# Exact FP4 codes for five of eleven down groups in a decoder layer: two matmul passes instead of three, and a rescale of the PSUM sum on VectorE

## The chip, the cores and the metric

The kernel runs on one core of one Trainium2 chip. The metric is the device time of the whole program in microseconds (us); below, PE is TensorE, DVE is VectorE, ACT is ScalarE, POOL is GpSimd and SP is SyncE, whose queue here issues every DMA.

## The reference

One decoder layer for x of shape (8, 256, 512), with three parts. The third part is the one that the change touches.

```
attention (linear, sigma = elu + 1, with a memory M, z)  -> x1 = layernorm(x + out)
Toeplitz convolution of k*v products of ctx, times q     -> x2 = layernorm(x1 + out)
ffn:
  vals = FP4_LUT[4-bit codes]                # 0, .5, 1, 1.5, 2, 3, 4, 6 and their negatives
  w    = vals * scale[group of 128 inputs, output]
  h    = silu(x2 @ w_gate.T) * (x2 @ w_up.T) # 1408 hidden values = 11 groups of 128
  y    = h @ w_down.T                        # 512 outputs
  y    = y * rsqrt(mean(y^2) + 1e-6);  out = layernorm(x2 + y)
```

A down weight is thus an FP4 code times a scale that is shared by the 128 hidden values of one group and differs for each of the 512 outputs.

## The kernel before

**Precision by passes.** TensorE multiplies fp16. An fp32 value is split into a high and a low fp16 part. For gate and up the weights are kept as exact FP4 codes in fp16 (`wg_hi`), so each product takes two passes (`x2_hi`, `x2_lo`), and between the four input groups ACT multiplies the sum that stands in PSUM by the ratio of two scales (`rescale_sums`, steps `rsI_P`). For down the scaled weight itself is split into `wd_hi` and `wd_lo`, and each group takes three passes of 512 columns (lines 1297, 1298 and 1299): h_hi with wd_hi, h_hi with wd_lo, h_lo with wd_hi. All 11 groups of a token half add up in one PSUM bank without an interruption.

**Stages.** The tokens of the second and third part go in eight blocks of 256 (two halves of 128). The start stage does the attention of all tokens, prepares the weights (33 tiles: POOL unpacks one, `wsN`; PE flips it, `wN`; ACT writes the high part, `whN`; for down tiles DVE writes the low part, `wlN`), and already runs the body of the first block. Then the body runs for it = 2 to 7, and a last body ends the program. A body works on the convolution of block it, on the ffn of block it-1, and on the rest of the ffn of block it-2.

**Orders.** Each engine runs its steps in an order written out as a string; an engine waits at a step until its semaphores are there, and everything behind it in the string waits with it. The body's orders are `PE_ORDER`, `DVE_ORDER`, `ACT_ORDER`, `POOL_ORDER`; `START_...` and `LAST_...` are those of the start stage and of the last body. The step names that matter here:

- PE: `gI_P` gate and up sums of hidden group I, input group P (4 matmuls of 256 columns); `cU` convolution unit U (3, 6, 9 or 12 matmuls of 288 columns), `d0 d1` the units 0 and 1 of the next block; `yT_I` down group I of token half T (T = 1 belongs to the block before); `w1_I` the same for half 1 in the last body; `ct`, `rt`, `xt` flips of 128x128 blocks.
- DVE: `tmU` products with a convolution unit, five instructions (from line 239); `lk`, `ln` the low part of the kv products (line 216); `kq` a transpose (line 223); `guI` hidden values (line 1201); `bsT`, `bnT`, `nmT`, `xtT` residual sum, statistics, normalisation and low part of x2; `aT`, `bT`, `eT` mean square, residual with statistics, and final normalisation (lines 1207, 1216 to 1224, 1232).
- ACT: `rsI_P`, `guI` (silu), `hhI` (high part of h), `hoT` (copy of x2), `nT` (squares of y).
- POOL: `hlI` (low part of h), `pr`, `pn` (kv products from line 197), `tr` (sums of the terms).

**Waits around the change.** `cU` waits until `tm` of unit U-2 has emptied its bank. `g0_0` waits for both `xt` of DVE. `d0` waits for `ln`. `yT_I` waits for `hlI` and, for I = 0, for `bT` of the block before. `hh` may overwrite a group of h once the down matmuls of the block before have read it.

## Time and profile before

| | |
|---|---|
| median of 3 runs | 537.16 us (536.99 to 537.49) |
| span of the profiled execution, first to last instruction | 535.3 us |
| PE busy | 508.7 us (95%), 3676 instructions |
| ACT busy | 415.7 us (78%) |
| POOL busy | 394.7 us (74%) |
| DVE busy | 374.4 us (70%), 1145 instructions |
| mean granted TensorE clock | 0.995 of full speed |

The profile gives of its own execution's time only the span; the median of the runs lies 1.9 us above it. Times of a trace count from the first instruction. A matmul's duration runs to the modelled end of its pipeline, and the next one starts before that, so what a matmul costs a full PE is the distance from its start to the next start. The same holds, in a smaller degree, for short instructions of DVE and ACT.

In this trace the start stage takes 0 to 176.1 us, the bodies it = 2 to 7 start at 176.10, 226.93, 278.14, 329.34, 380.54 and 431.74, and the last body runs from 481.92 to the last matmul's end at 525.22; then the last rows are normalised and stored.

### The profile page before, as it was taken

What the parts mean: (1) busy time and instruction counts of PE and PEld (TensorE: products, weight loads), DVE (VectorE), ACT (ScalarE), POOL (GpSimd) and SP (SyncE); (2) the same over time, 40 slices, a digit from 0 to 9 for tenths busy, and PEclk for the clock granted to TensorE, in tenths of its full rate; (3) what the DMA queues carried; (4) which work ended last, traced back from release to release, by engine and by line L of the source; (5) the groups of instructions that cost most, each with busy time, mean ns of one, the idle gap of its engine ahead of it and who ended that gap; (6) DMA issues with size and microseconds to landing.
All of it is one profiled execution on the core that took longest, in us unless ns stands there. A gap on an engine that the chain in (4) does not pass through costs nothing.

```text
span 535.3 us, 11768 instructions
## 1 busy us (share of the span) xinstructions
PE 508.7 (95%) x3676; PEld 377.6 (71%) x3676; DVE 374.4 (70%) x1145; ACT 415.7 (78%) x994; POOL 394.7 (74%) x449
## 2 busy tenths in 40 slices
PE   8888899998999999999999999999999999999992
PEld 5676787777785777677767776777677767765660
DVE  2886668988787667776777776768777777763223
ACT  4577875277999788788888897889788877788981
POOL 2768864994898499769968995899589859871231
PEclk9999999999999999999999999999999999999997
DMA  8713776443250862032104210411040111001001
GB/s 224 203 39 63 169 142 180 128 80 99 87 112 24 159 127 86 23 100 79 60 1 117 59 59 0 118 59 59 13 130 14 39 33 49 0 1 42 1 21 39
DMA packets 66146, 40.63 MB, mean 76 GB/s; under 512 B 37882, under 2 KB 55418, under 8 KB 66106
## 3 DMA queue, kind: packets, MB, share of 16 engines
q1 hardware_dynamic: 66106, 40.13, 29.6%
...
## 4 chain that ended last, share of the span: by engine, by line
PE 36%; POOL 27%; issue 19%; ACT 5%; DVE 4%; SPq 4%; DMA 2%; POOLq 1%; DVEq 0%; ACTq 0%
POOL shared L297 9%; POOL h_lo L1102 5%; SPq L415 4%; POOL kv L197 3%; PE p_cv L137 3%; PE p_cv L139 3%; PE p_cv L138 3%; PE p_n L1299 3%; PE p_n L1297 3%; PE p_n L1298 3%; POOL shared L299 2%; PE p_x L1284 2%; PE p_x L1286 2%; PE p_qk L1284 2%; PE p_qk L1286 2%
## 5 line engine op out<-in xcount | busy, mean ns | idle before, releaser
L1102 POOL TENSOR_TENSOR h_lo<-w,h_hi 128x256 f16<-128x256 f32 x88 | 73.6, 842 | 44.6 <-ACT h_hi L1151 43.0
L137 PE MATMUL p_cv<-kv_hi,toe 128*128 128x288 f16 x320 | 91.6, 286 | 1.3 <-DVE shared L257 1.3
L139 PE MATMUL p_cv<-kv_hi,toe 128*128 128x288 f16 x320 | 91.5, 286 | 0.0
L138 PE MATMUL p_cv<-kv_lo,toe 128*128 128x288 f16 x320 | 91.5, 286 | 0.0
L1134 ACT ACTIVATE p_qk<-p_qk,rescale 128x256 f32<-128x256 f32 x192 | 78.3, 451 | 12.5 <-PE p_qk L1286 11.9
L297 POOL TENSOR_TENSOR shared<-shared 128x1024 f32<-128x1024 f32 x32 | 76.8, 2399 | 8.9 <-DVE shared L257 8.8
L1134 ACT ACTIVATE p_x<-p_x,rescale 128x256 f32<-128x256 f32 x192 | 78.4, 452 | 6.2 <-PE p_x L1286 6.0
L1134 ACT ACTIVATE p_s<-p_s,rescale 128x256 f32<-128x256 f32 x144 | 59.0, 456 | 11.2 <-PE p_s L1286 11.1
L1297 PE MATMUL p_n<-wd_hi,h_hi 128*128 128x512 f16 x176 | 66.8, 379 | 0.0
L1298 PE MATMUL p_n<-wd_lo,h_hi 128*128 128x512 f16 x176 | 66.7, 379 | 0.0
L1299 PE MATMUL p_n<-wd_hi,h_lo 128*128 128x512 f16 x176 | 66.7, 379 | 0.0
L1284 PE MATMUL p_qk<-x_hi,wg_hi 128*128 128x256 f16 x256 | 63.0, 273 | 3.6 <-DVE x_lo L285 2.1
L1284 PE MATMUL p_x<-x_hi,wg_hi 128*128 128x256 f16 x256 | 62.9, 273 | 0.7 <-ACT p_x L1134 0.2
L1286 PE MATMUL p_x<-x_lo,wg_hi 128*128 128x256 f16 x256 | 62.8, 273 | 0.0
L1286 PE MATMUL p_qk<-x_lo,wg_hi 128*128 128x256 f16 x256 | 62.8, 273 | 0.0
L239 DVE TENSOR_TENSOR shared<-p_cv,qv 128x128 f32<-128x128 f32 x128 | 36.1, 282 | 32.4 <-PE p_cv L139 31.8
L216 DVE TENSOR_TENSOR kv_lo<-kv,kv_hi 128x1152 f16<-128x1152 f32 x32 | 52.6, 1642 | 3.4 <-ACT kv_hi L180 3.4
L242 DVE TENSOR_TENSOR shared<-p_cv,qv 128x128 f32<-128x128 f32 x128 | 49.7, 388 | 0.0
L299 POOL TENSOR_TENSOR shared<-shared 128x512 f32<-128x512 f32 x32 | 47.7, 1492 | 2.5
L1284 PE MATMUL p_s<-x_hi,wg_hi 128*128 128x256 f16 x192 | 47.1, 273 | 0.9 <-ACT p_s L1134 0.9
L1286 PE MATMUL p_s<-x_lo,wg_hi 128*128 128x256 f16 x192 | 47.1, 273 | 0.0
L180 ACT CAST kv_hi<-kv 128x1152 f16<-128x1152 f32 x32 | 37.3, 1166 | 10.9 <-POOL kv L208 7.2
...
## 6 DMA issues: line engine op xcount, KB each, us to landing
...
```

Of the source, the lines that this page charges most:

```text
L137: nc.tensor.matmul(dst, hi, kh, start=(mb == 0), stop=False)
L138: nc.tensor.matmul(dst, hi, kl, start=False, stop=False)
L139: done = nc.tensor.matmul(dst, lo, kh, start=False, stop=(mb == lb))
L297: nc.gpsimd.tensor_tensor(T[:, :, 0:256], T[:, :, 0:256], T[:, :, 256:512], ALU.add).then_inc(cv.tree, 1)
L299: nc.gpsimd.tensor_tensor(T[:, :, 0:128], T[:, :, 0:128], T[:, :, 128:256], ALU.add).then_inc(cv.tree, 1)
L1102: nc.gpsimd.tensor_tensor(h_lo[:, i, :], h32[:, i % 2, :], h_hi[:, i, :], ALU.subtract).then_inc(h_low, 1)
L1134: done = nc.scalar.activation(sums, sums, ACT.Copy, scale=rescale[:, p - 1, part * GI + i:part * GI + i + 1])
L1284: nc.tensor.matmul(dst, whi, cv.x2_hi[:, k, :], start=(k == 0 and part == 0), stop=False, skip_group_check=True)
L1286: done = nc.tensor.matmul(dst, whi, cv.x2_lo[:, k, :], start=False, stop=True, skip_group_check=True)
L1297: nc.tensor.matmul(p_y[t][:], h_hi[:, i, c], wd_hi[:, i, :], start=(i == 0), stop=False)
L1298: nc.tensor.matmul(p_y[t][:], h_hi[:, i, c], wd_lo[:, i, :], start=False, stop=False)
L1299: done = nc.tensor.matmul(p_y[t][:], h_lo[:, i, c], wd_hi[:, i, :], start=False, stop=(i == GI - 1))
```

## The change

For the down groups 0 to 4 (`EX = 5`) the weight stays an exact FP4 code. The pass with `wd_lo` is gone for them. Since the codes carry no scale, the sum in PSUM has to be brought from the scale of one group to that of the next: DVE multiplies the whole bank (128x512) by a tile of ratios, once after each of the groups 0 to 4, in a new step `sT_I` (`ST_I` in the last body), and `yT_I` for I = 1 to 5 waits for it. The last of these factors is the scale of group 4 itself, so from group 5 on the sum is in true units.

```diff
+        def rescale_down(f, t, i):
+            dve.wait_ge(y_part[t], f * EX + i + 1)
...
+            nc.vector.tensor_tensor(p_y[t][:], p_y[t][:], keep["early"][:, i * D:(i + 1) * D], ALU.mult).then_inc(y_rescaled[t], 1)
         def down(f, t, i):
...
+            if 0 < i <= EX:
+                pe.wait_ge(y_rescaled[t], f * EX + i)
+            nc.tensor.matmul(p_y[t][:], h_hi[:, i, c], wd_hi[:, i, :], start=(i == 0), stop=False,
+                             skip_group_check=True)
+            if i >= EX:
+                nc.tensor.matmul(p_y[t][:], h_hi[:, i, c], wd_lo[:, i - EX, :], start=False, stop=False,
+                                 skip_group_check=True)
+            done = nc.tensor.matmul(p_y[t][:], h_lo[:, i, c], wd_hi[:, i, :], start=False,
+                                    stop=(i < EX or i == GI - 1), skip_group_check=True)
+            if i < EX:
+                done.then_inc(y_part[t], 1)
```

The ratios are made in the start stage by four small DVE instructions (`dr0`), written to memory element by element by one DMA (`rw0`), and read back to all 128 partitions by another (`rl0`, 1.3 MB):

```diff
+        def down_ratios():
+            dve.wait_ge(scales_kept, 2)
+            nc.vector.tensor_scalar(dn_abs[:], sc_d[:, 0:EX], 0.0, NO_SCALE, ALU.is_equal, ALU.mult).then_inc(
...
+            nc.vector.reciprocal(dn_rec[:], dn_abs[:, 1:EX]).then_inc(ratios_made, 1)
...
+            elif name == "rw":
+                sp.wait_ge(ratios_made, 4)
+                sp.dma_start(ratio_rows.rearrange("g (t p) -> p g t", p=P), dn_abs[:],
+                             allow_slow_non_contiguous=True).then_inc(ratios_stored, 16)
+            elif name == "rl":
...
+                sp.dma_start(early[:, 0:EX * D].rearrange("p (g d) -> p g d", g=EX), bass.AP(ratio_rows.tensor, 0, [[0, P], [D, EX], [1, D]])).then_inc(
+                    keep["in_ratio"], 16)
```

For the five weight tiles 22 to 26 the start stage treats codes as it does for gate and up: POOL copies bytes instead of multiplying by the scale, PE flips one 128x128 block instead of four, and DVE has no low part to make (`wl22` to `wl26` are gone). Two waits that keep order inside one buffer are added, in `deviations` (ACT) and `add_residual` (DVE). The tile of ratios takes over the space of buffers that only the start stage uses.

All order strings are written anew. Those of a body, where the steps are most often run:

```diff
-    PE_ORDER = ("y1_0 g0_0 g1_0 y1_1 g0_1 y1_2 ct0 g1_1 g0_2 y1_3 y1_4 g2_0 g0_3 c2 g1_2 g3_0 c3 y1_5 g2_1 g1_3 g3_1 "
...
-                "g8_2 y0_2 g9_0 y0_3 g10_0 g8_3 g9_1 y0_4 g10_1 g9_2 d0 rt1 y0_5 g10_2 g9_3 y0_6 d1 g10_3 xt0 y0_7 "
-                "y0_8 y0_9 xt1 y0_10").split()
-    DVE_ORDER = ("tm0 tm1 gu0 lk1 tm2 tm3 gu1 tm4 tm5 gu2 lk2 tm6 tm7 tm8 gu3 tm9 tm10 lk3 tm11 gu4 a1 tm12 gu5 tm13 "
-                 "kq0 tm14 tm15 b1 gu6 gu7 ln kq1 bs0 bn0 bs1 bn1 gu8 nm0 gu9 nm1 gu10 xt0 xt1 a0 b0 e1 e0").split()
+    PE_ORDER = ("g0_0 g1_0 y1_0 g0_1 g2_0 g1_1 ct0 g0_2 g1_2 y1_1 g0_3 c2 g2_1 g3_0 y1_2 c3 g2_2 g3_1 g1_3 "
+                "c4 c5 g3_2 y1_3 g2_3 c6 g4_0 g5_0 g3_3 y1_4 c7 y1_5 g4_1 g5_1 y1_6 g4_2 c8 c9 y1_7 y1_8 "
+                "y0_0 g5_2 g4_3 y1_9 g6_0 y1_10 g5_3 c10 c11 g7_0 g6_1 ct1 c12 g8_0 g7_1 c13 c14 g6_2 g7_2 "
+                "c15 g8_1 y0_1 g6_3 g7_3 g8_2 y0_2 g9_0 g10_0 rt0 y0_3 g9_1 g8_3 g10_1 y0_4 rt1 g9_2 g10_2 "
+                "y0_5 g9_3 xt0 g10_3 y0_6 y0_7 y0_8 y0_9 xt1 y0_10 d0 d1").split()
+    DVE_ORDER = ("s1_0 tm0 tm1 gu0 s1_1 tm2 lk1 s1_2 tm3 tm4 gu1 tm5 gu2 s1_3 s1_4 lk2 tm6 tm7 tm8 kq0 tm9 "
+                 "s0_0 gu3 lk3 gu4 a1 gu5 tm10 tm11 tm12 tm13 b1 tm14 tm15 s0_1 gu6 gu7 s0_2 bs0 s0_3 bn0 "
+                 "s0_4 bs1 nm0 gu8 bn1 gu9 gu10 nm1 xt0 ln e1 xt1 a0 b0 kq1 e0").split()
```

In the start stage `fs0` (the gate and up scale factors) moves on DVE from behind `dn0` of the first attention tile to behind `o3` of the fourth; on SP `toe0` moves ahead of `st2`, and `rw0` stands between `st3` and `xq0`. In the last body `ho0` moves on ACT from the first step to near the end; behind the last gate and up step `g10_3`, PE has nine `w` and `y` steps in the old order and ten in the new, as these ends show:

```diff
-               "g10_1 g8_3 g9_2 w1_4 g10_2 w1_5 g9_3 w1_6 g10_3 w1_7 y0_6 w1_8 w1_9 w1_10 y0_7 y0_8 y0_9 y0_10").split()
-    LAST_ACT = ("ho0 rs0_1 rs1_1 rs2_1 tl rs0_2 rs1_2 rs0_3 rs2_2 rs1_3 gu0 rs2_3 hh0 gu1 rs3_1 gu2 rs4_1 rs3_2 hh1 "
...
+    LAST_PE = ("y1_0 g0_0 g1_0 g0_1 g1_1 g0_2 g1_2 g2_0 y1_1 g0_3 g1_3 g2_1 y1_2 g3_0 g4_0 g2_2 y1_3 y0_0 "
...
+               "y0_4 g9_1 g10_1 w1_3 y0_5 g8_2 g9_2 g10_2 w1_4 g8_3 y0_6 g9_3 g10_3 w1_5 w1_6 w1_7 w1_8 w1_9 "
+               "w1_10 y0_7 y0_8 y0_9 y0_10").split()
```

## Rows read from the trace of the kernel before

**Rows 1.** Windows: start stage, body 6, body 7, last body; busy us of each engine.

```profile
0.00:176.10 176.10, 162.35 (x1102) 127.19 (x1103) 131.65 (x387) 125.18 (x272) 128.43 (x164) 1.00 0.50 120
380.54:431.74 51.20, 51.02 (x388) 37.71 (x386) 38.47 (x121) 42.89 (x106) 42.90 (x45) 1.00 0.17 51
431.74:481.92 50.18, 49.57 (x370) 35.65 (x369) 35.17 (x118) 39.92 (x101) 39.70 (x41) 1.00 0.08 22
481.92:525.22 43.30, 41.93 (x276) 26.07 (x274) 12.47 (x28) 36.18 (x98) 10.08 (x16) 1.00 0.07 19
```

**Rows 2.** Timeline of PE: end of body 5, begin of body 6 (start, duration, us).

```profile
379.45 0.60 PE L102 MATMUL p_ct<-ident,shared 128*128 128x128 f32 x4
379.89 0.38 PE L1297 MATMUL p_n<-wd_hi,h_hi 128*128 128x512 f16 x1
...
380.32 0.38 PE L1299 MATMUL p_n<-wd_hi,h_lo 128*128 128x512 f16 x1
380.54 0.38 PE L1297 MATMUL p_n<-wd_hi,h_hi 128*128 128x512 f16 x1
...
381.53 0.28 PE L1284 MATMUL p_qk<-x_hi,wg_hi 128*128 128x256 f16 x1 [0.18 <-DVE x_lo L285]
...
381.98 0.27 PE L1284 MATMUL p_x<-x_hi,wg_hi 128*128 128x256 f16 x1
...
387.63 0.30 PE L137 MATMUL p_cv<-kv_hi,toe 128*128 128x288 f16 x1
...
388.75 0.27 PE L1284 MATMUL p_x<-x_hi,wg_hi 128*128 128x256 f16 x1
```

**Rows 3.** Groups of DVE's instructions by line and shape, whole run (busy us, mean ns).

```profile
L216 DVE TENSOR_TENSOR kv_lo<-kv,kv_hi 128x1152 f16<-128x1152 f32 x32 | 52.6, 1642 | 3.4 <-ACT kv_hi L180 3.4
...
L285 DVE TENSOR_TENSOR x_lo<-p_ct,x_hi 128x512 f16<-128x512 f32 x16 | 11.0, 690 | 12.8 <-ACT x_hi L184 12.7
...
L265 DVE TENSOR_TENSOR shared<-p_ct,xr 128x512 f32<-128x512 f32 x16 | 10.7, 671 | 4.5 <-PE p_ct L102 4.5
```

**Rows 4.** Timeline of DVE: end of body 5, begin of body 6.

```profile
371.60 0.65 DVE L265 TENSOR_TENSOR shared<-p_ct,xr 128x512 f32<-128x512 f32 x1
...
378.51 0.69 DVE L285 TENSOR_TENSOR x_lo<-p_ct,x_hi 128x512 f16<-128x512 f32 x1 [0.22 <-ACT x_hi L184]
380.71 0.69 DVE L285 TENSOR_TENSOR x_lo<-p_ct,x_hi 128x512 f16<-128x512 f32 x1 [1.50 <-ACT x_hi L184]
381.46 0.15 DVE L1207 TENSOR_SCALAR ms<-ss 128x1 f32<-128x1 f32 x1
...
384.24 0.55 DVE L1232 TENSOR_SCALAR fin<-z,mv,rs 128x512 f32<-128x512 f32 x1
385.31 1.40 DVE L1232 TENSOR_SCALAR fin<-z,mv,rs 128x512 f32<-128x512 f32 x1 [0.53 <-POOL rs L1098]
386.63 0.28 DVE L239 TENSOR_TENSOR shared<-p_cv,qv 128x128 f32<-128x128 f32 x1
...
388.37 0.46 DVE L1201 SCALAR_TENSOR_TENSOR w<-p_qk,c_up,w 128x256 f32<-128x256 f32 x1
```

**Rows 5.** Timeline of POOL at the same place.

```profile
385.16 1.27 POOL L197 TENSOR_TENSOR kv<-kT 128x512 f32<-128x512 f32 x1
```

**Rows 6.** Timeline of SP's queue in the start stage.

```profile
72.21 8.19 SPq L415 DMA_DIRECT2D x_blocks<-z  x8
...
83.34 4.90 SPq L426 DMA_DIRECT2D xq<-x_blocks  x2
```

**Rows 7.** Timeline of DVE in the start stage.

```profile
17.02 0.20 DVE L682 TENSOR_SCALAR sc_abs<-sc_g 128x88 f32<-128x88 f32 x1
...
19.88 0.60 DVE L767 SCALAR_TENSOR_TENSOR o<-p_n,coef,loc 128x128 f32<-128x128 f32 x2
...
87.06 0.71 DVE L223 STREAM_TRANSPOSE qv<-xq 128x512 f32<-128x512 f32 x1 [1.14 <-DMA xq<-x_blocks]
```

**Rows 8.** Timeline of ACT: begin of the last body.

```profile
484.50 0.62 ACT L1156 COPY x2hold<-shared 128x512 f32<-128x512 f32 x1 [1.69 <-DVE z L1216]
```

More of the change, by code:

```diff
@@ L39 @@
 RING = 5
+EX = 5
 LATE = ("y1", "n1", "a1", "b1", "e1")
@@ L1037, in periods @@
         "y_done", "y_squared", "y_used", "rr_made", "rs3_made", "fin_made", "y_steps"))
+    y_part, y_rescaled = ([sem(f"{n}{t}") for t in range(GT)] for n in ("y_part", "y_rescaled"))
     def before(i):
@@ new lines, in decoder_layer @@
+    START_SYNC = ("x3 x4 cx2 st0 x5 cx3 tw0 st1 cx4 toe0 x6 st2 st3 rw0 xq0 xq1 xq2 x7 cx5 toe1 xr0 xq3 xr1 "
+                  "toe2 xr2 st4 xq4 toe3 rl0 cx6 toe4 xr3 xq5 cx7 st5 st7 st6 toe5").split()
+    START_PE = ("ze0 Xa0 iw0 Xb0 iw1 iw2 iw3 Q0 V0 S0 M0 Xa1 Xb1 N0 iz0 Q1 T0 f0 w0 Oa0 w1 Ob0 Xa2 w2 S1 w3 "
[9 rows of a table added]
+                "+xt1 +y0_8 +y0_9 +y0_10 +d0 +d1").split()
+    START_DVE = ("ze0 is0 sg0 mk0 ig0 u0 dn0 o0 u1 ra0 sg1 rb0 bm0 mk1 u2 dn1 bn0 dr0 o1 u3 ra1 nb0 rb1 bm1 "
[7 rows of a table added]
+                 "+xt1 +kq1 +a0 +b0 +e0").split()
@@ new lines, in decoder_layer @@
+    ACT_ORDER = ("rv0 rs0_1 rs1_1 rs0_2 rs1_2 rs0_3 rs2_1 tl gu0 rs1_3 hk1 rs2_2 hh0 rs3_1 ho0 ct0 rs3_2 "
+                 "rs2_3 gu1 gu2 rs3_3 rs4_1 hk2 gu3 hh1 hh2 rs5_1 rs4_2 rs5_2 rv1 rs4_3 rs5_3 hk3 hh3 gu4 n1 "
+                 "gu5 hh4 rs6_1 rs7_1 hh5 kn rs6_2 rs7_2 rs8_1 rs6_3 ho1 rs7_3 ct1 rs8_2 gu6 gu7 rs8_3 rs9_1 "
+                 "rs10_1 hh6 hh7 rs9_2 rs10_2 gu8 rs9_3 rs10_3 hh8 gu9 gu10 hh9 xt0 hh10 xt1 n0").split()
+    POOL_ORDER = ("pr1 hl0 pr2 tr0 pr3 hl1 hl2 tr1 hl3 pn hl4 hl5 a1 tr2 tr3 bn0 hl6 hl7 hl8 bn1 hl9 b1 hl10 "
+                  "a0 b0").split()
@@ new lines, in decoder_layer @@
+    LAST_PE = ("y1_0 g0_0 g1_0 g0_1 g1_1 g0_2 g1_2 g2_0 y1_1 g0_3 g1_3 g2_1 y1_2 g3_0 g4_0 g2_2 y1_3 y0_0 "
[3 rows of a table added]
+               "w1_10 y0_7 y0_8 y0_9 y0_10").split()
+    LAST_DVE = ("s1_0 s1_1 gu0 gu1 s1_2 s1_3 s0_0 s1_4 gu2 gu3 gu4 a1 s0_1 b1 gu5 s0_2 S1_0 gu6 gu7 S1_1 "
+                "s0_3 S1_2 s0_4 e1 S1_3 S1_4 gu8 gu9 gu10 A1 B1 a0 b0 E1 e0").split()
+    LAST_ACT = ("tl rs0_1 rs1_1 rs0_2 rs1_2 rs0_3 rs1_3 rs2_1 gu0 gu1 rs2_2 hh0 rs3_1 rs4_1 rs2_3 rs3_2 "
+                "rs4_2 gu2 rs3_3 rs4_3 hh1 hh2 gu3 gu4 rs5_1 hh3 hh4 rs6_1 rs7_1 rs5_2 rs6_2 n1 rs7_2 rs5_3 "
+                "rs6_3 gu5 rs7_3 hh5 gu6 gu7 rs8_1 hh6 rs9_1 rs10_1 hh7 rs8_2 rs9_2 rs10_2 rs8_3 rs9_3 "
+                "rs10_3 gu8 gu9 hh8 ho0 gu10 hh9 hh10 N1 ho1 n0").split()
```

107 lines of the change are left out of this document (61 added, 46 removed), and 51 rows, old and new, of tables (LAST_PE, PE_ORDER, START_ACT, START_DVE).

## The prediction

> **What bounds the kernel now.** I read the windows by stage first. In body 6 PE is busy for 51.02 of 51.20 us, DVE for 38.47, ACT for 42.89 and POOL for 42.90 [rows 1]. So a body is PE's: nothing that another engine saves shows, and every us taken from PE shows, as long as the others keep up. The start stage is different: PE is busy for 162.35 of 176.10 us, so 13.75 us are waits. In the last body PE has 41.93 of 43.30 us and ACT, which first waits, 36.18 [rows 1].
>
> What a pass costs a full PE is read in PE's timeline, not from a duration. A pass lasts 0.38 us to the end of its pipeline, but from 380.32 to 380.54 the next one starts after 0.22 us, and the three from 379.89 take 0.65 us in all [rows 2]. I use 0.215. In the same rows a `g` step costs 0.44 (381.53 to 381.98, rounded down), a flip step 0.44 (379.45 to 379.89), and the nine matmuls of `c2` 1.12, or 0.122 each (387.63 to 388.75) [rows 2].
>
> **What is taken from PE.** A body has ten steps `yT_0` to `yT_4`, one pass less in each: 10 x 0.215 = 2.15 us. There are six bodies: 12.9 us. The last body loses 15 passes, 3.2 us. The start stage loses the five of `y0` (1.1 us) and, in five weight tiles, three of four flips (15 x 0.11 = 1.65 us). All in all 80 passes and 15 flips, 18.9 us. Were PE the bound throughout, this would be the gain, and a body would take 51.2 - 2.15 = 49.05 us.
>
> **What is put on DVE.** Ten multiplies of 128x512 a body. Before has none that writes PSUM. The nearest rows are two with one PSUM input, 671 ns (line 265) and 690 ns (line 285) [rows 3]; from one start to the next an instruction costs some 0.08 less (two convolution units, ten instructions, take 386.63 to 388.37, 0.87 a unit [rows 4]). I take 0.61 behind another instruction and 0.69 where PE waits. DVE's busy time becomes 38.5 + 6.1 to 6.9 = 44.6 to 45.4 of 49.05 us: 91 to 93%. By share it still fits. But each multiply is between two steps of PE, and DVE's queue is strict, so I follow the two queues at the two places where DVE has least room.
>
> **First place: the begin of a body.** DVE must do `a0 b0 kq1 e0` of the block before, then `s1_0`, `tm0`. In the trace DVE ends `xt1` at 381.40, PE starts `g0_0` at 381.53, DVE starts `a0` at 381.46, and `tm0` follows at 386.63, 5.2 us behind `a0` [rows 2, 4]. Of that, 1.4 us is `e0`, which takes 0.55 elsewhere (the instruction before it in the rows) but starts at 385.31, inside POOL's 1.27 us product at 385.16 [rows 4, 5]. The new order has `kq1` in place of `e1`, in the time of a wait for POOL, and the same neighbours on POOL, so the collision stays: `s1_0` starts 4.8 us behind `g0_0` (4.0 without the collision). It ends at 5.5 (4.7). In the new `PE_ORDER` seven `g` steps, a two-pass step and a flip stand ahead of `y1_1`, 7 x 0.44 + 0.43 + 0.44 = 3.95 us. So PE stands still for 1.6 us there (0.75 without the collision). Then `tm0` ends at 6.4, before `c2` needs it. `c5` needs `tm3`, with `tm0` to `tm3`, `gu0`, `lk1`, `s1_1`, `s1_2` ahead; at 0.87, 0.4 (0.46 less 0.08), 1.64 and 0.61 each this can add up to 0.3. In the old order DVE had no `s1_0`, and `tm0` was done at about 387.55, just ahead of `c2` at 387.63 [rows 2, 4]: there was no room to give away.
>
> The Trainium skill, SBUF — State Buffer, "SBUF: two separate sides", says that the port pair shared by VectorE and GpSimd is an exclusive lock that whichever starts first holds for a whole instruction, for VectorE operations in a two-port mode or with two SBUF inputs. The row of `e0` agrees. By this rule the multiply, with one input from PSUM, is never held by POOL and the sums stay as they are; no row of before shows a multiply beside POOL, and were it held as `e0` was, at 0.85 us for a third of the ten, DVE would need 48 us and the slower rival below would be the likeliest.
>
> **Second place: the end of a body.** From `bs0` to the end of `gu10` DVE took 371.60 to 378.51, 6.9 us, of which 0.6 waits that a later start removes: 6.3. The new order puts `s0_3` and `s0_4` into this chain (1.2), then `xt0` 0.65, `ln` 1.64 (the mean of line 216, between 1.3 alone and 2.0 beside POOL), `e1` 0.5, `xt1` 0.69 [rows 3, 4]: 11.0 us, with 0.3 for the flip's end and the way back 11.3. In the old order `ln` and `e1` were not there, and DVE sat idle for 1.50 us ahead of `xt1` [rows 4]. PE from the end of `rt0` to `g0_0` has two two-pass steps, six of three passes, seven `g`, three flips, `d0` and `d1`: 0.86 + 3.88 + 3.08 + 1.32 + 1.10 = 10.2 us. So PE waits up to 1.1 us; with `ln` at 1.3 and the shorter `nm` it is 0.3. I take 0.6.
>
> A body is then 49.05 + 1.6 + 0.6 less 0.3 for small waits that these replace (0.2 of them ahead of `g0_0` [rows 2]) = 50.95 us. Five bodies (it = 2 to 6) gain 0.25 each, 1.2 in sum. Body 7 has no `ln`, `kq` or `d` steps: the second place falls away, and it gains 0.55. The bounds of a body are 49.75 (0.7 and 0.3) and 52.0 (1.9 and 1.1).
>
> **Start stage.** PE's 2.7 us count in part, since it waits for 13.75. On the good side `fs0` moves: its five instructions stood from 17.02 to 19.88 between the denominators and `o0` [rows 7], on the chain of the first tile, 2.9 us; `dr0` comes in its place later with four such small ones, 1 us or, where POOL is in the way as for `fs0`, 3. The five low parts that go save DVE 5 x 0.6 = 3, and `s0_0` to `s0_4` add 3. `s0_1` to `s0_4` stand in a row, with PE steps between them that are too short (`g10_0` only, 0.44, against 1.4 for the multiply and its way): some 1 us. On the bad side is `rw0`. It is 2560 elements of 4 bytes. The nearest rows are the eight issues of `x_blocks`, 4096 rows of 128 bytes, that hold SP for 8.19 us; at this price `rw0` holds it 5.1 us, and it stands ahead of `xq0`, which started at 83.34, about 3 behind the stores, and for which DVE waited 1.14 us at 87.06 [rows 6, 7]. So 2 us of 5.1 lie under the stores' landing, and up to 3 reach `kq0`, and with it the first convolution sums on DVE and POOL. `rl0` is issued long before `s0_0`, which stands late in the body that ends the start stage; it costs nothing, and some 11 us (1.3 MB at the stage's 120 GB/s [rows 1]) if that cover were gone. Together: -2.7 - 2.9 + 1 + 1 + 1.4 (half of what may reach `kq0`) = -2.2, between -5.5 and +3.
>
> The Trainium skill, DMA: Bandwidth & Descriptors, "Rules for kernel authors", says that a last dimension that isn't contiguous becomes one descriptor for each element. It speaks against `rw0`, and agrees with pricing it by count; were it priced by its 10 KB, it would cost nothing, and the start stage would gain 1.4 us more.
>
> **Last body.** ACT goes first to `ho0`, waits for `b0` until 484.50, and only then starts on the rescales, though it was free 1.69 us earlier [rows 8]. With `ho0` (0.5) moved they can start some 2.2 us earlier; the stall at `y1_1` takes 0.7 back (no POOL work collides here). From there ACT has one step after another, so the 3.2 us of PE give nothing more. At the end PE has ten three-pass steps behind `g10_3` instead of nine, +0.65. Net -1 to -1.5, I take -1.5; between -3 and +0.5. The 10 us after the last matmul stay.
>
> **Sum.** Profiled span 535.3 - 1.2 - 0.55 - 2.2 - 1.5 = 529.85; with the 1.86 by which the median of the runs lies above it, 531.7 us.
>
> **The rivals.**
> *PE stays the bound (20%).* DVE's 91% is spread well enough, `e0` misses POOL, `ln` falls short. All 18.9 us but 2.5 in the last body come: 521. For it speaks that every engine stays under 93%; against it the 5.2 us between `a0` and `tm0`, longer than the 3.95 that PE now has.
> *The gain is eaten exactly (13%).* A body of 51.2, and start and last body cancel each other: 537.2.
> *DVE's chain becomes longer than PE's (24%), slower.* Both places at their upper bound: `e0` behind a POOL product, `ln` at 2.0 beside another, `c5` late. A body of 52.0 costs 5 x 0.8 + 0.5 = 4.5 us, less 2.2 for the start: 539.5. It decides at a sum of 2.45 us of PE stall in a body; I have 2.2. This closeness is the weak point of the forecast.
> *The ratio store delays the convolution (within my case).* All 3 us and its descriptors in front of `xq0`: +1.6, 533.3.
>
> **Chances and range.** My case, 527 to 536, has 43%; PE-bound 20% (518 to 526). Faster by over 0.2% (under 536.1; 0.2% is about what a measurement of this kernel tells from no change) is these two: 63%. Within 0.2%: 13%. Slower: 24%. The range from 522.5 to 540 takes in most of both neighbours and leaves out some 2 in 10. The predicted time is 531.7.
>
> **What would show it.** A body of 50.95 us (period from `g0_0` to `g0_0`) with PE busy for some 48.9; PE waits for line `rescale_down` ahead of `y1_1`, once a body, and for `xt1` or `ln` at its end; DVE near 45 us a body; multiplies of 0.69. A body under 49.5, with PE idle under 0.5, makes PE-bound right; over 51.3 the slower case. `xq` landing later than 87 shows `rw0`. What would make me wrong is a multiply into PSUM far from 0.69, or steps of ACT and POOL that I took as ready and that are not.

## The result, and the profile after

The changed kernel takes 568.3 us (median of 4 runs, 565.13 to 572.55) against 537.33 (median of 4) for the one before on the same chip: 1.058 times as long, 95% interval 1.053 to 1.064. The forecast was 531.7, between 522.5 and 540.0. The prediction was wrong, in sign too.

The windows by stage of the kernel after, cut at the first step of each stage (start stage; body 5, like the other middle ones; body 7; last body to the end of the span):

```profile
0.00:197.67 197.67, 163.47 (x1082) 126.65 (x1083) 133.01 (x392) 125.09 (x273) 129.13 (x164) 0.96 0.49 111
357.48:410.97 53.49, 50.63 (x378) 35.70 (x376) 44.31 (x131) 42.69 (x106) 41.12 (x45) 1.00 0.21 59
464.44:513.57 49.13, 47.01 (x357) 33.87 (x355) 40.81 (x127) 38.66 (x97) 37.63 (x41) 1.00 0.08 22
513.57:564.90 51.33, 40.11 (x267) 24.41 (x264) 25.61 (x52) 37.00 (x100) 12.01 (x20) 0.93 0.10 26
```

Against [rows 1] the start stage is 21.6 us longer. A middle body takes 53.49 us instead of 51.20; the first one lost 2.0 and the four behind it 9.1 together. Body 7 gains 1.05. The last body takes 51.33 to the end of the span where before needed 535.3 - 481.92 = 53.38, so it gains 2.05. The sum, 21.6 + 11.1 - 1.05 - 2.05 = 29.6 us, is the difference of the spans (564.9 and 535.3). PE issues ten matmuls less in a body, as meant (378 for 388), and DVE is busy for 44.31 us, close to the forecast. What is new is that PE no longer works through its body: its own steps add up to some 48.6 us of start-to-start distances, and 4.85 us are waits.

Where the start stage waits is seen on three queues. SP's timeline (issues of DMAs):

```profile
81.18 7.10 SPq L420 DMA_DIRECT2D x_blocks<-z  x8
...
88.32 0.81 SPq L470 DMA_DIRECT2D ratio_rows<-dn_abs  x1
94.72 12.54 SPq L431 DMA_DIRECT2D xq<-x_blocks  x3
```

DVE's timeline:

```profile
90.31 0.59 DVE L803 SCALAR_TENSOR_TENSOR o<-p_n,coef,loc 128x128 f32<-128x128 f32 x2
106.09 0.71 DVE L224 STREAM_TRANSPOSE qv<-xq 128x512 f32<-128x512 f32 x1 [15.19 <-DMA xq<-x_blocks]
```

Then the table of DMA issues (KB each, median us from issue to landing):

```profile
ratio_rows<-dn_abs SPq DMA_DIRECT2D x1, 10.0 KB, 17.6
```

The windows of the same stretch (the columns are those of [rows 1]):

```profile
80.00:94.70 14.70, 13.13 (x96) 11.57 (x94) 9.09 (x18) 8.86 (x17) 7.44 (x12) 0.99 0.59 86
94.70:100.00 5.30, 0.00 (x0) 0.00 (x0) 0.00 (x0) 0.00 (x0) 0.00 (x0) 0.75 0.27 18
100.00:106.10 6.10, 0.00 (x0) 0.00 (x0) 0.01 (x1) 0.00 (x0) 0.00 (x0) 0.50 0.72 65
```

`kq0` ran at 87.06 in before and waited 1.14 us [rows 7]; now it runs at 106.09 and waits 15.19. All five engines stand still for 11.4 us. The ratio store was issued in 0.81 us, but its 10 KB landed 17.6 us later, at 105.9, and `xq`, issued behind it, came only then. The issue of `xq` was itself late: `xq` waits for the stores of x1 to have landed, and it starts 6.4 us behind the end of their last issue (88.28 to 94.72), where before needed 2.9 (80.40 to 83.34 [rows 6]).

The body's waits are read in PE's timeline of body 5. These are the three largest kinds, for a multiply (`y1_1`), for the normalised x2 (flip `xt0`), and for GpSimd's low parts (`y0_9`, `y0_10`):

```profile
362.96 0.39 PE L1350 MATMUL p_n<-wd_hi,h_hi 128*128 128x512 f16 x1 [0.97 <-DVE p_n L1251]
...
403.80 0.65 PE L103 MATMUL p_ct<-ident,shared 128*128 128x128 f32 x4 [0.35 <-DVE shared L280]
...
407.15 0.39 PE L1350 MATMUL p_n<-wd_hi,h_hi 128*128 128x512 f16 x1 [0.32 <-POOL h_lo L1142]
...
409.21 0.39 PE L1350 MATMUL p_n<-wd_hi,h_hi 128*128 128x512 f16 x1 [0.81 <-POOL h_lo L1142]
```

From start to start, less the step's own work, these cost 1.13, 0.51, 0.48 and 0.97 us. The last one has its cause on GpSimd, whose low part of h takes 1.59 us there:

```profile
404.58 0.67 POOL L1142 TENSOR_TENSOR h_lo<-w,h_hi 128x256 f16<-128x256 f32 x1 [1.19 <-ACT h_hi L1193]
...
407.57 1.59 POOL L1142 TENSOR_TENSOR h_lo<-w,h_hi 128x256 f16<-128x256 f32 x1
```

while DVE runs `ln` and, behind it, `e1`:

```profile
407.28 1.35 DVE L217 TENSOR_TENSOR kv_lo<-kv,kv_hi 128x1152 f16<-128x1152 f32 x1
408.55 0.90 DVE L1281 TENSOR_SCALAR fin<-z,mv,rs 128x512 f32<-128x512 f32 x1
```

The other 1.76 us are seven waits of 0.15 to 0.28 (1.54 together), ahead of gate steps and units, and 0.22 spread over the rest.

### The profile page after: what moved, and what is told of

Its sections match the earlier page's. It is cut to its first block, busy times and chain, and to the rows that moved or that the text cites. A ratio compares the mean times of both kernels' runs of the same rounds, so it can differ in the third digit from the quotient of the medians.

```text
span 564.9 us, 11773 instructions
## 1 busy us (share of the span) xinstructions
PE 502.7 (89%) x3581; PEld 364.0 (64%) x3581; DVE 419.8 (74%) x1224; ACT 414.1 (73%) x994; POOL 384.7 (68%) x449
## 4 chain that ended last, share of the span: by engine, by line
POOL 29%; PE 20%; issue 20%; DVE 11%; SPq 8%; DMA 6%; ACT 3%; POOLq 1%; DVEq 0%; ACTq 0%
POOL shared L298 9%; SPq L420 7%; POOL h_lo L1142 6%; DMA xq<-x_blocks 3%; POOL kv L198 3%; POOL shared L300 3%; POOL shared L305 2%; DMA x_blocks<-ring 2%; POOL kv L208 2%; POOL kv L203 2%; PE p_cv L138 2%; PE p_n L1350 2%; PE p_cv L140 2%; PE p_cv L139 2%; PE p_n L1355 2%
## 5 line engine op out<-in xcount | busy, mean ns | idle before, releaser
L1142 POOL TENSOR_TENSOR h_lo<-w,h_hi 128x256 f16<-128x256 f32 x88 | 66.8, 770 | 51.2 <-ACT h_hi L1193 51.2
L1174 ACT ACTIVATE p_qk<-p_qk,rescale 128x256 f32<-128x256 f32 x192 | 79.5, 463 | 4.9 <-PE p_qk L1337 4.0
L1251 DVE TENSOR_TENSOR p_n<-p_n,early 128x512 f32<-128x512 f32 x80 | 55.0, 692 | 14.9 <-PE p_n L1355 14.9
L543 POOL COPY w<-shared 128x256 uint8<-128x256 uint8 x54 | 36.4, 831 | 22.2 <-DVE shared L764 14.7
L198 POOL TENSOR_TENSOR kv<-kT 128x512 f32<-128x512 f32 x32 | 41.1, 1285 | 14.5 <-DVE kv_lo L217 14.5
L138 PEld LDWEIGHTS p_cv<-kv_hi,toe 128*128 128x128 f16 x320 | 31.5, 98 | 29.5 <-DVE shared L258 18.0
L243 DVE TENSOR_TENSOR shared<-p_cv,qv 128x128 f32<-128x128 f32 x128 | 49.6, 388 | 0.0
```

Of the source, the lines that this page charges most:

```text
L138: nc.tensor.matmul(dst, hi, kh, start=(mb == 0), stop=False)
L198: ops.tensor_tensor(flat[:, 0:4].rearrange("p i (r j) -> p i r j", j=4), kb[:, :, 0:4].rearrange("p r (i a) -> p i r a", a=1).to_broadcast ...
L1142: nc.gpsimd.tensor_tensor(h_lo[:, i, :], h32[:, i % 2, :], h_hi[:, i, :], ALU.subtract).then_inc(h_low, 1)
L1174: done = nc.scalar.activation(sums, sums, ACT.Copy, scale=rescale[:, p - 1, part * GI + i:part * GI + i + 1])
L1251: nc.vector.tensor_tensor(p_y[t][:], p_y[t][:], keep["early"][:, i * D:(i + 1) * D], ALU.mult).then_inc(y_rescaled[t], 1)
```

## The experiments

Fourteen kernels ran. "Body" is the period of the first step from body 6 to body 7 in the profiled execution. Before measured 536.5 to 537.3 us beside them.

| kernel | what it has | body, us | start stage ends | time, us | ratio to before |
|---|---|---|---|---|---|
| before | | 51.20 | 176.1 | 537.3 | |
| after | all of the change | 53.47 | 197.7 | 568.3 | 1.058 |
| rw_early | store of the ratios early | 53.46 | 189.1 | 557.6 | 1.038 (1.034 to 1.041) |
| rw_rows | store in 128 runs | 53.47 | 186.9 | 555.7 | 1.034 (1.032 to 1.036) |
| no_multiply | rw_early, no multiply | 51.10 | 188.1 | 543.7 | 1.011 (1.010 to 1.013) |
| orders_alone | new orders, old arithmetic | 52.77 | 184.8 | 554.3 | 1.031 (1.027 to 1.035) |
| start_before | start in before's order | 53.42 | 183.0 | 553.8 | 1.033 (1.031 to 1.036) |
| ln_early | rw_early, `ln` moved | 53.76 | 187.1 | 558.9 | 1.043 (1.038 to 1.049) |
| half_multiply | rw_early, half the columns | 51.83 | 185.0 | 546.4 | 1.020 (1.016 to 1.024) |
| no_upper | rw_early, 5 of 10 multiplies | 52.48 | 188.2 | 551.1 | 1.026 (1.024 to 1.029) |
| own_layout | before's orders, change put in | 54.56 | 185.7 | 560.6 | 1.044 (1.042 to 1.045) |
| own_layout2 | the same, steps moved | 53.67 | 182.6 | 556.1 | 1.037 (1.035 to 1.039) |
| three_groups | own_layout2, 3 groups of 11 | 53.90 | 177.6 | 553.6 | 1.031 (1.030 to 1.033) |
| mended | new body, steps moved at its waits | 58.11 | 183.2 | 584.1 | 1.087 (1.085 to 1.089) |
| mended2 | mended, two steps moved again | 54.15 | 184.0 | 557.7 | 1.039 (1.036 to 1.041) |
| mended2_rows | mended2, store in runs | 54.19 | 179.8 | 553.5 | 1.030 (1.028 to 1.032) |

The two orders begin a body with different steps: the new bodies with `g0_0`, before's with `y1_0` (also in own_layout, own_layout2 and three_groups). In before `g0_0` follows at 176.75, 0.65 us behind `y1_0`, so across the two orders the ends of the start stage compare to 0.65 us; rw_early and ln_early, whose start stages are the same, ended theirs at 189.1 and 187.1, so a difference of 2 us in this column is within what one execution can show. The first four kernels ask what the ratio store, the multiplies and the new orders each cost by themselves.

**rw_early.** The store `rw0` moved on SP, `... cx2 rw0 st0 ...` for `... st3 rw0 xq0 ...`.

> The changed kernel with one step moved on SP: the ratio store rw0 goes ahead of st0, where SP otherwise waits and the ratios have been ready for some 10 us. Theory 1 (the store's 2560 elements hold the queue, and xq0 behind it, for 18 us): the start stage becomes some 15 us shorter, DVE's wait of 15.2 us for xq is gone, 552 to 555 us in all; st0 may start up to 3 us later. Rival (xq0 is late because the attention of the start stage is, and its stores land late): no more than 5 us are won, 563 or more.

557.6 us: 10.7 us came back (8.6 in the start stage of the profiled execution), the bodies stayed. The number lies between theory and rival, nearer the theory: the store's place cost some 11 us, but `xq` is not late by the store alone.

**rw_rows.** The store at the change's place, in another shape.

```diff
-  sp.dma_start(ratio_rows.rearrange("g (t p) -> p g t", p=P), dn_abs[:], allow_slow_non_contiguous=True) ...
+  sp.dma_start(bass.AP(ratio_rows.tensor, 0, [[EX * 4, P], [1, EX * 4]]), dn_abs[:].rearrange("p g t -> p (g t)")) ...
```

> The changed kernel with the ratio store left at its place between st3 and xq0, but written as 128 runs of 80 bytes instead of 2560 of 4 bytes. The tile of ratios that is read back then holds its values in another order, so the output is not the reference's. If the count of elements is the cost: the store lands in 2 to 3 us instead of 17.6 and the kernel takes 550 to 554 us, like rw_early or a little less. If any DMA at this place delays xq0 (a fixed cost, the order of the queue): over 560.

555.7 us, 12.6 less than after and 1.7 above the range of the theory. The same 10 KB from the same place in 128 runs of 80 bytes landed in 3.0 us instead of 17.6:

```profile
ratio_rows<-dn_abs SPq DMA_DIRECT2D x1, 10.0 KB, 3.0
```

So it is the number of pieces that costs, not the bytes and not the wait of SP for the ratios. The Trainium skill, DMA: Bandwidth & Descriptors, "Rules for kernel authors", says that a last dimension that isn't contiguous becomes one descriptor for each element. The DMA packets of the two whole executions, of after and of this kernel, agree with it: they differ by 2432, which is 2560 less 128.

```profile
DMA packets 68866, 41.95 MB, mean 74 GB/s; under 512 B 40474, under 2 KB 58010, under 8 KB 68698
```

```profile
DMA packets 66434, 41.95 MB, mean 76 GB/s; under 512 B 38042, under 2 KB 55578, under 8 KB 66266
```

**no_multiply.** The 80 steps `sT_I` and PE's waits for them taken out of rw_early.

> As rw_early, and the 80 multiplies on DVE and PE's waits for them are left out (the output is then not the reference's); two passes for five groups and all orders stay. A body takes 53.47 us in the changed kernel and PE's steps add up to 48.7. Theory 2 (the multiplies and the waits that they bring make up the 4.8 us of PE stall in a body): a body of 49 to 49.5 us, 520 to 526 us in all. Rival (the new orders stall by themselves, on POOL's low parts and ACT's rescales): a body of 51 to 52.5 us, 537 or more.

543.7 us: the multiplies cost 14.0 us, 2.36 in a body. But the body of 51.10 us did not come near the 49 that ten passes less allow; the rival's bound was met, and 2.5 us of PE's waits in a body are there without any multiply. They are not the same waits: those for `h_lo` 9 and 10 and the one ahead of `xt0` are gone, and the largest left is 0.63 us, ahead of `d0` for `ln`.

**orders_alone.** Before's arithmetic (three passes, no ratios) with the order strings of the change. `wl22` to `wl26`, which those strings no longer have, stand behind `mk4`, `o4` and `rb4`, and the two waits that the change adds for its orders are kept.

> The kernel before, with all order strings of the changed one (without the multiplies, dr0, rw0 and rl0, with wl22 to wl26 put in, and with the two added waits in deviations and add_residual): three passes everywhere. It prices the new layout alone. If the layout is sound and only the multiplies and the ratio store cost: 537 plus or minus 3, a body of 51 to 51.5 us. If the start stage's new layout costs by itself (st0 starts 10 us later in the changed kernel, st3 ends 8 us later): start stage 3 to 8 us longer, 541 to 548 us.

554.3 us, more than either expectation. With nothing but the new orders (and the places that I gave `wl22` to `wl26` in them) the kernel loses 17 us. The start stage loses 8.7 (8.0 from `g0_0` to `g0_0`), and a body 1.57. The body's largest wait is the one ahead of the last pass, so it needs no multiply:

```profile
446.93 0.39 PE L1299 MATMUL p_n<-wd_hi,h_hi 128*128 128x512 f16 x1 [0.76 <-POOL h_lo L1103]
```

In the start stage the delay is there early. ACT's step `nm0`, the normalisation of the first tile of x1, stands ahead of `wh7` in before's order and behind `xa3`, `vk2` and `xb3`, steps of the third and fourth tile, in the new one. The timelines of ACT, of before and of this kernel:

```profile
36.39 1.52 ACT L631 ACTIVATE ring<-ring,shift,rs 128x512 f32<-128x512 f32 x2
```

```profile
45.45 1.52 ACT L632 ACTIVATE ring<-ring,shift,rs 128x512 f32<-128x512 f32 x2
```

The first store of x1, which waits for it on SP, moves with it:

```profile
37.94 0.39 SPq L410 DMA_DIRECT2D x_rows<-ring  x1
```

```profile
46.99 0.39 SPq L410 DMA_DIRECT2D x_rows<-ring  x1
```

That is 9.05 us; at `xq0` 6.5 are left (89.80 for 83.34). No kernel moved `nm0` alone, so that it is the cause of the 8.7 us at the end of the stage is not shown.

Four kernels (before, orders_alone, no_multiply, rw_early) are a path on which each body differs from the one before it by one thing: 51.20 + 1.57 (orders) - 1.67 (ten passes, with 2.15 of work) + 2.36 (ten multiplies) = 53.46. Differences along a path add up by themselves; taken in another order, the parts could be other ones. Nor does it say that the orders are bad for an arithmetic that they were not tried with.

**start_before.** The start strings of before, with `dr0`, `rw0`, `rl0` and `+s0_0` to `+s0_4` put in, the new bodies.

> The start stage's layout alone put back: the first stage follows before's orders on all five engines, with what the change adds set into them (ratios worked out after the first context statistics, their store ahead of the first x1 store, the five multiplies between the late terms). The bodies and the last body stay as the change has them. Theory (the new order of the start stage costs by itself, some 8 us, seen as 185.7 against 176.1 us for the first pass of the first body when the new orders ran with the old arithmetic): the first down pass of body 1 falls from 189.9 us (store of the ratios early, new start) to 180 to 183, and the time from 557.6 to 547 to 551. Rival (the start stage is late from the change itself, the store and the multiplies, and the orders matter little): above 555.

The start stage fell from 189.1 to 183.0 us and the profiled span from 556.1 to 550.0. The median fell by 3.8 only, between the expectation and the rival. Part of the start's loss is thus the order; 6.2 us against `g0_0` of before (176.75) remain, and are taken up below.

**ln_early.**

```diff
-  s0_1 gu6 gu7 s0_2 bs0 ... nm1 xt0 ln e1 xt1 a0 b0
+  s0_1 gu6 gu7 ln s0_2 bs0 ... nm1 xt0 e1 xt1 a0 b0
```

> Against the kernel with the early ratio store (557.6): in the bodies alone, VectorE's low part of the next context window (1.35 us beside the last hidden groups) stands right behind the multiplication of group 7, its place in before, instead of ahead of the last finish of a body. Theory (this operation and the finish behind it hold up GpSimd's last low part h_lo 10, which took 1.59 us there against 0.67 elsewhere, and PE waits 0.97 us for it): PE's wait ahead of pass y0_10 goes, the body falls from 53.46 to 52.4 to 52.9 us and the time to 551.5 to 555. Rival (what is late is the whole chain of VectorE behind the five multiplies, so that the 1.35 us only move to another place in it): body 53.3 to 53.9, time 556.5 to 561.

The theory's mechanism is right and its gain is not there. `h_lo` 10 takes 0.67 us again and PE's wait for it is gone:

```profile
453.80 0.67 POOL L1142 TENSOR_TENSOR h_lo<-w,h_hi 128x256 f16<-128x256 f32 x1
```

But `ln` now stands ahead of `s0_2` and takes 1.93 us there, beside GpSimd's sums, for 1.35:

```profile
442.65 1.93 DVE L217 TENSOR_TENSOR kv_lo<-kv,kv_hi 128x1152 f16<-128x1152 f32 x1
```

PE waits for that multiply at `y0_3`:

```profile
445.25 0.39 PE L1350 MATMUL p_n<-wd_hi,h_hi 128*128 128x512 f16 x1 [1.37 <-DVE p_n L1251]
```

The body became 0.3 us longer. The rival holds.

**half_multiply.** Columns 0 to 255 only, `p_y[t][:, 0:D // 2]`.

> Against the kernel with the early ratio store (557.6; the body 53.46 with 128x512 multiplies, 51.10 with none): each of the 80 multiplies covers half of the columns of the sum, so the output is not the reference's. Theory (the multiplies cost by VectorE's time, 0.69 us each, which delays the chain at the body's end; 10 of them cost 2.36 us of body): half the elements should take about 0.36 to 0.42 us each and give back nearly half of it: body 52.2 to 52.6, time 548 to 552. Rival (they cost by the handshake, two semaphores and a turn to another engine, whatever their size): body above 53.0, time above 554.

Body 51.83, 546.4 us: both below the range of the theory, and far from the rival's. The groups of DVE's instructions by line and shape, of after and of this kernel:

```profile
L1251 DVE TENSOR_TENSOR p_n<-p_n,early 128x512 f32<-128x512 f32 x80 | 55.0, 692 | 14.9 <-PE p_n L1355 14.9
```

```profile
L1251 DVE TENSOR_TENSOR p_n<-p_n,early 128x256 f32<-128x256 f32 x80 | 33.8, 425 | 18.5 <-PE p_n L1355 18.4
```

Ten multiplies of 425 ns lengthen the body by 0.73 us, ten of 692 ns by 2.36. So the first 4.25 us of DVE's time cost 0.17 us per us, and the next 2.67 us cost 0.61 per us: it is time that counts and not the handshake alone, and most of the first part disappears in holes of DVE's order.

**no_upper.** The multiplies `s1_I` of the upper half left out of rw_early.

> Against the kernel with the early ratio store (557.6, body 53.46; 51.10 without any multiply): only the five multiplies of the upper half of a chunk (which stand in the first third of a body) are left out, the five of the lower half stay, so that the output is not the reference's. Theory (the cost lies where VectorE is dense, at the body's end with the lower half's): only the wait of 1.13 us at the second upper pass goes, and of it 0.2 to 0.5 comes back at the first late terms: body 52.5 to 52.9, time 550 to 554. Rival (the multiplies cost alike wherever they stand, 2.36 us over 10): body 52.2 to 52.4, time 548 to 550. A third (the upper ones cost nothing, PE would wait for the late terms there anyway): body above 53.1.

Body 52.48: the five lower multiplies cost 1.38 us and the five upper ones 0.98. The wait of 1.13 us at `y1_1` is gone and 0.51 us came in its place at `c2`, for the `tm0` that it waits for. The three waits at the end (0.51, 0.47, 0.97) are all there. The body lies at the edge between theory and rival, the time of 551.1 us within the theory's range; they are not parted.

**own_layout.** The change in before's strings for start and bodies. In the body, PE's `y1_2` to `y1_5` and `y0_3`, `y0_4` stand one to several steps later, and DVE has:

```diff
-  tm0 tm1 gu0 lk1 tm2 tm3 gu1 tm4 ... tm15 b1 gu6 gu7 ln kq1 bs0 bn0 bs1 ... xt0 xt1 a0 b0 e1 e0
+  tm0 tm1 s1_2 gu0 lk1 s1_3 tm2 tm3 gu1 s1_4 tm4 ... tm15 s0_0 b1 s0_1 gu6 gu7 s0_2 ln s0_3 bs0 bn0 s0_4 bs1
+  ... xt0 xt1 a0 S1_0 b0 kq1 e1 S1_1 e0
```

> The change's whole arithmetic (5 groups in two passes, 80 multiplies) in before's orders of all stages but the last body, with as few moves as the multiplies need: start as in the run with before's start, in the bodies the passes of the five groups one or two gate steps apart, two multiplies of the upper half in the holes of the end chain, the turn of q behind it. Theory (the new layout is what lost most; before's order has 12.7 us of idle VectorE a body, and PE's work is 2.2 us a body less): body 50.3 to 51.8 us, time 531 to 541. Rival (any layout has the 7 us of multiplies a body pressing on VectorE's chain, which was dense from 416 to 430 us in body 6 of before): body 52.5 or more, time above 545.

560.6 us, the rival's side. PE waits four times a body for a multiply, the longest at `y1_2`:

```profile
407.70 0.39 PE L1350 MATMUL p_n<-wd_hi,h_hi 128*128 128x512 f16 x1 [1.94 <-DVE p_n L1251]
```

**own_layout2.** The same with the steps set to meet: on DVE `S1_1` ahead of `e1`, `s1_2` behind `gu0`, `kq1` between `xt0` and `xt1`; on PE `y1_2` and `y0_2` to `y0_5` one or two steps later.

> The change in before's orders once more, with PE's passes and VectorE's multiplies set to meet. In the first try (560.6 us, body 54.56) PE waited 2.10, 0.88, 0.39 and 0.80 us a body for a multiply that stood too late in VectorE's order, and 2.73 us once in the start stage. Now the second multiply of the upper half follows the residual at once, the third follows hidden group 0, passes y0_1 to y0_5 stand one or two gate steps later, the turn of q stands in the wait between the two low parts of x2 (1.50 us of idle VectorE). Theory (what the multiplies cost is their place; VectorE has room for them at 45 of 50 us a body): body 50.2 to 51.3, time 531 to 541. Rival (VectorE's chain from the last context terms to the low parts of x2 is full, and every multiply in it comes back as a wait somewhere): body above 52.3, time above 545.

No pass waits long for a multiply any more, and the body is still 53.67 us. The waits have gone to what stands behind the multiplies on DVE, `tm0` and the hidden value of a group:

```profile
403.79 0.30 PE L138 MATMUL p_cv<-kv_hi,toe 128*128 128x288 f16 x1 [0.98 <-DVE shared L258]
...
437.38 0.28 PE L1335 MATMUL p_qk<-x_hi,wg_hi 128*128 128x256 f16 x1 [1.11 <-DVE w L1243]
```

From start to start they cost 1.15 and 1.27 us.

**three_groups.** own_layout2 with `EX = 3`, without `sT_3` and `sT_4`, with `wl25` and `wl26`.

> The same orders with the change on three of the eleven down groups instead of five: 48 passes and 48 multiplies less or more than before instead of 80. PE has 1.29 us a body less than before instead of 2.16, VectorE 4.1 us more instead of 6.9. Theory (each multiply of the end chain costs more than its pass gives, 0.69 us of a full VectorE against 0.22 us of PE): three groups beat five in the same orders, body 0.3 to 1.5 us below that of the run with five, time 3 to 10 us less. Rival (PE is still what bounds the body, so that fewer removed passes mean a longer body): 0.3 to 0.9 us a body above it, time 2 to 6 us more.

The body is 53.90, not below the 53.67 with five groups. The theory falls; 0.23 is just less than the rival's bound. The same two waits are both there (1.14 and 1.27 us), as both stand behind multiplies that three groups still need. What made this kernel 2.5 us faster is its start stage, 5.0 us shorter. In it the store has 1536 values for 2560, and it landed in 10.7 us.

**mended.** start_before with the new body changed at each of its waits (and `+y0_1`, `+kq1` and `S1_0` moved alike in the start stage):

```diff
-  s1_0 tm0 tm1 ... tm15 s0_1 gu6 gu7 s0_2 bs0 s0_3 ... nm1 xt0 ln e1 xt1 a0 b0 kq1 e0        (DVE)
+  tm0 tm1 ... tm15 s0_1 e1 gu6 gu7 s0_2 ln bs0 s0_3 ... nm1 xt0 xt1 a0 kq1 b0 S1_0 e0
-  y0_3 g9_1 g8_3 g10_1 y0_4 rt1 g9_2 g10_2 y0_5 g9_3 xt0                                     (PE)
+  y0_3 g9_1 g8_3 g10_1 rt1 g9_2 y0_4 g10_2 g9_3 y0_5 xt0
-  tr2 tr3 bn0 ... bn1 hl9 b1 hl10                                                            (GpSimd)
+  tr2 tr3 b1 bn0 ... bn1 hl9 hl10
```

> The change with its own body orders mended at the places where PE waited in the body of 53.46 us (1.13 for the second multiply of the upper half, 0.51 ahead of the flip of x2, 0.47 and 0.97 for GpSimd's last low parts), and the start stage in before's orders. Moved: the first multiply of the upper half to right behind the residual of the lower one, the turn of q into the wait ahead of it, the last finish of the upper half from the body's end to behind the late terms (GpSimd's part of it with it), the low part of the next context window ahead of the statistics, passes y0_4 and y0_5 two and one gate steps later. Theory (each of these is a wait by place, and VectorE at 44.3 of 53.5 us a body has room for all): body 51.0 to 52.2 us, time 539 to 547. Rival (the waits only move along VectorE's chain): body 53 or more, time above 549, as the two tries in before's orders gave 54.56 and 53.67.

584.1 us, 30 more than start_before. One step did most of it: `e1` needs GpSimd's `b1`, which now stood behind its two longest sums, and all that DVE had behind `e1` waited too:

```profile
460.93 0.55 DVE L1281 TENSOR_SCALAR fin<-z,mv,rs 128x512 f32<-128x512 f32 x1 [4.90 <-POOL rs L1138]
```

PE waits 4.77 us for it at `g9_0`, and its clock falls with the wait: the granted clock of the body is 0.97, where the bodies of the other kernels have 1.00, and the matmuls behind that wait take 0.1 us more each, 1.5 together.

```profile
417.94:476.05 58.11, 52.19 (x379) 36.89 (x377) 43.71 (x132) 42.70 (x105) 40.59 (x45) 0.97 0.16 45
```

This run says nothing on the theory. **mended2** takes the error out: GpSimd's `b1` between `tr2` and `tr3`, `e1` behind `ln`.

> The mended orders with the one wait of 4.9 us taken out (the last finish of the upper half stood ahead of GpSimd's step for it): GpSimd's step now stands ahead of its last long product, the finish behind the low part of the next context window. Theory (the waits of the change's own body are waits by place and go when the steps are moved): body 51.2 to 52.3 us instead of 53.46, time 541 to 547, so below the 553.8 us of the kernel with before's start alone, but still above before, whose body is 51.20 and whose start is 6 us shorter. Rival (the waits move along VectorE's chain and come back): body 53 or more, time above 549.

Body 54.15 us, 557.7 us: the rival. The waits for the second multiply and for `h_lo` 10 are gone, and two others stand in their place, at the flips `rt1` and `xt0`, for `bs0` and `nm0` (1.78 and 0.82 us from start to start):

```profile
445.02 0.32 PE L103 MATMUL p_ct<-ident,shared 128*128 128x128 f32 x1 [1.61 <-DVE shared L266]
...
448.92 0.32 PE L103 MATMUL p_ct<-ident,shared 128*128 128x128 f32 x1 [0.66 <-DVE shared L280]
```

**mended2_rows.** mended2 with the store of rw_rows.

> The same with the ratios stored as 128 runs of 80 bytes instead of 2560 single values of 4 bytes, so that they come back in a wrong order and the output is not the reference's. Theory (even early in the start stage the store holds up the transfers behind it: the DMA engines were 0.67 busy at 24 GB/s from 35 to 45 us, and the x tile that PE waits 3.3 us for comes late): 3 to 5 us less than mended2, the first pass of body 1 at 179 to 181 us. Rival (the early store lies beside idle queues, and what the start loses is the multiplies): within 1.5 us of mended2.

553.5 us, 4.2 less, all of it before the first body. The windows from 35 to 45 and from 45 to 55 us, of mended2 and of this kernel, show it in the last two columns, the share of the DMA engines and GB/s:

```profile
35.00:45.00 10.00, 8.51 (x55) 6.71 (x54) 9.16 (x19) 8.40 (x18) 9.35 (x13) 1.00 0.78 22
45.00:55.00 10.00, 9.11 (x57) 7.22 (x56) 5.07 (x16) 7.44 (x18) 8.14 (x13) 1.00 0.61 64
```

```profile
35.00:45.00 10.00, 8.25 (x52) 6.54 (x53) 9.53 (x19) 8.38 (x17) 8.78 (x12) 1.00 0.42 91
45.00:55.00 10.00, 9.10 (x55) 7.14 (x54) 4.89 (x17) 7.45 (x18) 8.14 (x13) 1.00 0.28 57
```

With the store in single values the engines are about twice as busy, and from 35 to 45 us they move a quarter of the bytes. SP's timeline shows it too, in the issue of the eight stores that stand behind the ratio store, again of mended2 and of this kernel:

```profile
38.28 17.45 SPq L420 DMA_DIRECT2D x_blocks<-ring  x8
```

```profile
38.84 7.33 SPq L420 DMA_DIRECT2D x_blocks<-ring  x8
```

Even placed early, the store costs 4.2 us in these orders; what is left of the start's loss against `g0_0` of before is 3.1 us, in a start stage that now has the multiplies.

## Why the prediction was wrong

The step that failed first, and by most, is the **start stage**: forecast -2.2 us with bounds of -5.5 and +3, measured +21.6. Within it the term for `rw0` was mis-sized. I priced it by SP's issue rows [rows 6], 5.1 us of SP, of which 3 could reach `kq0`, and put 1.4 into the sum. SP issued it in 0.81 us; what its own row of issue doesn't show is how long the pieces keep other transfers from landing, which was 17.6 us. Removing that (rw_rows) gives back 12.6 us, 10.8 of them in the start stage of the profiled execution. The second part is a term that the sum did not have: the new order of the stage by itself, 8.0 to 8.7 us with the old arithmetic. I had priced the steps that move one by one (`fs0`, `dr0`) and taken the rest of a reordered stage of 176 us as neutral. Of these `fs0` was mis-sized as well: its 2.9 us were to shorten the chain of the first tile, but `o0` starts at 19.81 us for 19.88, since it then waits for ACT:

```profile
19.81 0.61 DVE L803 SCALAR_TENSOR_TENSOR o<-p_n,coef,loc 128x128 f32<-128x128 f32 x2 [0.69 <-ACT loc L619]
```

And PE's 2.7 us, which by my own words count only in part, stand in the sum whole.

**The body** was forecast at 50.95 us (bounds 49.75 and 52.0) and took 53.49: 48.65 of PE's own steps, 1.13 at the first place, 1.96 at the second, 1.76 in small waits. By its steps:

- The passes: ten less in a body. The work is as forecast (48.65 us of PE's own steps; the 49.05 had 0.4 of before's small waits in it), but it was worth 1.67 us, not 2.15, as PE did not bind throughout.
- The multiply: 0.69 us, measured 692 ns over 80, and DVE's 44.31 us a body for 44.6 to 45.4. Right, a little under the range.
- First place, 1.6 us ahead of `y1_1`: right. I had `s1_0` start 4.8 us behind `g0_0` and end at 5.5; in the rows below it starts 4.72 us behind `g0_0` (410.98) and ends at 5.41, with `e0` at 1.40 us as before. PE reaches `y1_1` 1.52 us late, 1.13 at `y1_1` itself, once a body, for `rescale_down`, and 0.39 in two small waits ahead of it. But no_upper shows that 0.51 us would be there without the upper multiplies, at `c2` for `tm0`; in no_multiply it was 0.32.

```profile
410.79 0.15 DVE L1255 TENSOR_SCALAR ms<-ss 128x1 f32<-128x1 f32 x1 [0.75 <-ACT sq L1204]
411.61 0.75 DVE L1265 SCALAR_TENSOR_TENSOR z<-p_n,rr,x2hold 128x512 f32<-128x512 f32 x1 [0.66 <-POOL rr L1138]
...
414.38 1.40 DVE L1281 TENSOR_SCALAR fin<-z,mv,rs 128x512 f32<-128x512 f32 x1
415.70 0.69 DVE L1251 TENSOR_TENSOR p_n<-p_n,early 128x512 f32<-128x512 f32 x1
```

- Second place, 0.6 us at the end: mis-sized, and the wrong path. DVE's chain is as forecast: from `bs0` to the end of `xt1` 11.0 us, measured 10.97 (399.07 to 410.04). But what PE waits for is not its end: ahead of the next `g0_0`, which needs `xt1`, there is no wait. I had moved `ln` and `e1` only on DVE's own queue. Beside them GpSimd's `h_lo` 10 takes 1.59 us for 0.67, and the pass behind it waits 0.97; with the waits of 0.48 and 0.51 ahead of it the place costs 1.96 us. The wait at the last pass is there in orders_alone too (0.92), so it comes from the order and not from the multiplies alone. The rule on the shared port, which I had weighed for the multiply, held for the multiply (none of the 80 took over 0.70 us) and should have been carried to the other moved pair.
- "Less 0.3 for small waits that these replace": they were not replaced. The small waits are 1.76 us.

So the stall is 4.85 us in a body (4.45 if it is counted from 49.05) where the forecast had 2.2 and its own point of decision was 2.45. The rival that came nearest is "DVE's chain becomes longer than PE's"; its time of 539.5 was far too low, since it held the start stage at -2.2. The rival with PE as the bound is refuted, and so is the one by which the gain is eaten exactly.

Three small slips of the working change nothing in this: nine matmuls in 1.12 us are 0.124 each, not 0.122; the body's upper bound of 52.0 leaves out the 0.3 that the lower one subtracts; and the last body's terms (-2.2, +0.7, +0.65) add up to -0.85, not to the -1.5 that I took.

**Body 7** gained 1.05 (0.55 forecast, without bounds) and the **last body** 2.05 (1.5, within its bounds): right in sign. As the terms of the last body give 0.85, its nearness to 1.5 is in part luck.

Is it the layout or the multiplies? Both, on the path taken here: 1.57 us a body from the orders with the old arithmetic, 2.36 from the multiplies in the new orders. Five layouts with all the multiplies (after's, ln_early, own_layout, own_layout2, mended2) gave 53.5, 53.8, 54.6, 53.7 and 54.2 us, and mended 58.1. In the tries to mend one, a wait that was taken away came back behind another step of DVE. DVE's mean share of 83% hides two stretches where it has no idle time over 0.16 us: from `bs0` to the end of `xt1`, and from `b0` to `tm0` (411.61 to 416.30). Between them it waits 0.75 and 0.66 us, for ACT and for GpSimd, as the rows above show. The first stretch in the windows:

```profile
399.07:410.04 10.97, 9.49 (x64) 5.77 (x62) 10.44 (x19) 7.46 (x20) 7.33 (x10) 1.00 0.01 5
```

That no layout of the change beats 51.20 is not shown; none of mine did, and no kernel tried here was faster than before.

Open: which step of the reordered start stage costs its 8.0 to 8.7 us was not taken apart; `nm0` is where the delay is first seen. start_before gave back 6.1 in the trace and 3.8 in the median.
